# Token projection over pairs of rows with staggered softplus; patch filter with depthwise rows split between two engines

## The chip, the cores and the metric

The program runs on one core of one Trainium2 chip. The metric is device microseconds from start to end of one execution. The engines are TensorE (PE), VectorE (DVE), ScalarE (ACT), GpSimd (POOL) and SyncE (SP, which here issues nearly all DMAs). Each works through its own instructions in order; semaphores alone tie them together.

## The reference, cut to what matters

An image of 48 channels by 128x128 pixels goes through four layers, each `x = x + layer(group_norm(x))`: attention over all pixels, a patch filter, a selective scan and a box filter. The change touches the second layer and the first part of the third.

```python
# layer 1, patch filter: 48 -> 288 channels
y = einsum('oc,bchw->bohw', w_in, x)
f = rfft2(8x8 patches of y) * fft_mask;  y = irfft2(f)
y = depthwise 3x3 convolution of y (288 channels)
x1, x2 = split(y, 2)                      # 144 channels each
return einsum('oc,bchw->bohw', w_out, gelu(x1) * x2)
# layer 2, scan: a token is a 2x2 window, 192 numbers; 4096 tokens
Bm = tokens @ W_B.T + b_B;  Cm = tokens @ W_C.T + b_C
dt = softplus(tokens @ W_dt.T + b_dt);  delta = softplus(dt + b_dt)
# then the recurrence over tokens with delta, delta*u, Bm, Cm
```

## The kernel before, in words

**Group norm** (`group_norm`, used ahead of each layer): one `bn_stats` of VectorE per 512 pixels, two tiny matmuls, some tiny vector operations; it leaves scale and shift in `norm`. With `write_normalised` it also writes the normalised image to partitions 0 to 47 (`LO`) beside the original on 64 to 111 (`HI`). It is a block of its own: all engines meet at its start and at its end.

**Patch filter** (`patch_filter_layer`). After the norm, one block clears tiles on GpSimd and loads weights, a second prepares the mask and nine diagonal matrices (`diag`) on VectorE, and a third does the work. The image is worked off in 16 rows of patches (r), each in two halves (hf). For a half, `stage` (VectorE) writes normalised pixels to `staged_x`, TensorE transposes them (L739), VectorE copies them out (`x_t`, L920), TensorE applies the forward transform (L745, `ps_x`), ScalarE copies (`spec`, L810), TensorE mixes channels (L751, `ps_y`, four matmuls over two banks), VectorE multiplies by the mask (`ym`, L926), and TensorE transforms back (L758, `ps_i`) in three groups of channels: a and b of 128 and c of 48. ScalarE writes them to the slabs (`placed`, L824) with two rows of the slab above (`halos`, L831).
The depthwise convolution runs one row of patches later: group a (channels before the gelu) on TensorE, nine taps of 512 columns for each half (L770); groups b (128 channels, the gates) and c (the small third: 16 channels before the gelu and their 16 gates, on 48 partitions) on VectorE, each nine operations of 1024 elements (`taps`, L881, L883). `gates` multiplies gelu by gate, `output` multiplies by `w_out`, `add` adds to the image. VectorE's order is written out by hand: `iteration` gives away eight taps between a half's copy and its mask. A float32 matmul is two instructions in the profile.

**Token projection** (`project_tokens`). A block of norm with the normalised image written out; then a block in which GpSimd clears weight tiles, SP loads them and stores the image (`kept_image`), and then eight blocks of 512 tokens. A projection sums four matmuls, one for each place of the 2x2 window; eight projections a block (two halves of `dt`, two of `u`, four of `ps_b`). The softplus is |x|, exp(-|x|), ln(1+.), relu on ScalarE and an add on VectorE, done twice for each half, one after the other, through the same tiles. VectorE then splits delta and delta*u into three bfloat16 parts, and SP stores them (`parts`), from which the scan loads.

Of the kernel before, what the change touches and what calls it, by code (L numbers as in the profile page):

```python
# [19 lines left out]
BF16 = mybir.dt.bfloat16  # L20
# [70 lines left out]
def group_norm(nc, tag, image, gmean, norm, sems, write_normalised):  # L91


    with ExitStack() as ctx:
# [20 lines left out]
        def _(dve):  # L115
# [30 lines left out]
            if write_normalised:  # L146
                for px in quarters[:2]:
                    nc.vector.tensor_scalar(image[LO, px], image[HI, px], rstd, shift,
                                            ALU.mult, ALU.add).then_inc(normalised, 1)
                dve.wait_ge(normalised, written + 4)  # L150

# [480 lines left out]
PATCH = 8  # L632
HID = 3 * C
# [4 lines left out]
WP = W + 2  # L638


def patch_filter_layer(nc, image, gmean, norm, sems, ident, d):
# [5 lines left out]
    group_norm(nc, "gn1", image, gmean, norm, sems, False)  # L647
    with ExitStack() as ctx:
# [6 lines left out]
        dwa = n.sb("dwa", [P, 9])  # L655
        dwb = n.sb("dwb", [P, 9])
        dwc = n.sb("dwc", [SPAN, 9])
        diag = n.sb("diag", [P, 9, P])
        w_oa = n.sb("w_oa", [P, C])
        w_oc = n.sb("w_oc", [P, C])  # L660
# [6 lines left out]
        slab_c = n.sb("slab_c", [48, 2, SLAB, WP])  # L667
        gate_a = n.sb("gate_a", [P, 2, BLK])
        gate_c = n.sb("gate_c", [P, 2, BLK])
        acc_b = n.sb("acc_b", [P, PATCH, W])  # L670
        acc_c = n.sb("acc_c", [48, PATCH, W])
        ps_t = n.ps("ps_t", [P, 4, C])
# [4 lines left out]
        ps_o = n.ps("ps_o", [C, BLK])  # L677
        loaded, cleared, made = n.sem("loaded"), n.sem("cleared"), n.sem("made")
        staged, turned, turned_copied, spectrum, spectrum_copied, mixed, masked, inverted, placed, halo = (
            n.sem(s) for s in ("staged", "turned", "turned_copied", "spectrum", "spectrum_copied", "mixed", "masked",  # L680
                               "inverted", "placed", "halo"))
        conv_a, tap_b, tap_c, gelu_a, gelu_c, gated, product, added = (
            n.sem(s) for s in ("conv_a", "tap_b", "tap_c", "gelu_a", "gelu_c", "gated", "product", "added"))

        with nc.Block() as block:
            @block.sync
            def _(sp):
                pairs = ((fwd[:, :], d["fourier_fwd"]), (inv[:, :], d["fourier_inv"]),
                         (mask[0:64, :], d["mask"]), (mask[64:P, :], d["mask"]),
                         (mask2[0:64, :], d["mask_mirror"]), (mask2[64:P, :], d["mask_mirror"]),  # L690
                         (dwa[:, :], d["w_dw"][0:P, :]), (dwb[:, :], d["w_dw"][HID:HID + P, :]),
                         (w_oa[:, :], d["w_out"][0:P, :]))
                for dst, src in pairs:
                    sp.dma_start(dst, src).then_inc(loaded, 16)
                sp.wait_ge(cleared, 9)
                sp.dma_start(w_in[LO, :], d["w_in"]).then_inc(loaded, 16)
                sp.dma_start(dwc[0:REST, :], d["w_dw"][P:HID, :]).then_inc(loaded, 16)
                sp.dma_start(dwc[32:48, :], d["w_dw"][HID + P:2 * HID, :]).then_inc(loaded, 16)
                sp.dma_start(w_oc[32:48, :], d["w_out"][P:HID, :]).then_inc(loaded, 16)
                sp.wait_ge(loaded, 16 * 13)  # L700

            @block.gpsimd
            def _(pool):
                for t in (slab_a, slab_b, slab_c):
                    nc.gpsimd.memset(t[:, :, :, :], 0.0).then_inc(cleared, 1)
                nc.gpsimd.memset(gate_c[:, :, :], 0.0).then_inc(cleared, 1)
                nc.gpsimd.memset(w_oc[:, :], 0.0).then_inc(cleared, 1)
                nc.gpsimd.memset(acc_c[:, :, :], 0.0).then_inc(cleared, 1)
                nc.gpsimd.memset(dwc[:, :], 0.0).then_inc(cleared, 1)
                nc.gpsimd.memset(w_in[:, :], 0.0).then_inc(cleared, 1)  # L710
                nc.gpsimd.memset(spec[:, :, :], 0.0).then_inc(cleared, 1)

        with nc.Block() as block:
            @block.vector
            def _(dve):


                nc.vector.tensor_tensor(mask[:, :], mask[:, :], mask2[:, :], ALU.add).then_inc(made, 1)
                dve.wait_ge(made, 1)
                nc.vector.tensor_scalar(mask[:, :], mask[:, :], 0.5, None, ALU.mult).then_inc(made, 1)  # L720
                for t in range(9):
                    nc.vector.tensor_scalar(diag[:, t, :], ident[:, :], dwa[:, t:t + 1], None,
                                            ALU.mult).then_inc(made, 1)
                dve.wait_ge(made, 11)

        block = ctx.enter_context(nc.Block())
        rows_of = lambda slab, ph: slab[:, ph]
        final_rows = 1

        @block.tensor  # L730
        def _(pe):
            def transform(r, hf, first_work, second_work):

                q = r * 2 + hf
                pe.wait_ge(staged, q + 1)
# [1374 lines left out]
```

## Time and profile before

| | us |
|---|---|
| time, median of 3 runs | 8075.75 (8073.62 to 8077.5) |
| the profiled execution | 8077.16, its span 8075.4 |
| first and last mask of the patch filter | 3364.6 and 3890.3 |
| end of the second norm's statistics | 3976.6 |
| token projection's first matmul | 3994.6 |
| scan's first load issued | 4236.4 |

| stretch, us from the span's start | what it is |
|---|---|
| 0 to 3317 | attention |
| 3318 to 3342 | norm ahead of the patch filter |
| 3342 to 3948 | patch filter |
| 3948 to 3977 | norm ahead of the scan layer |
| 3977 to 4236 | token projection |
| 4236 to 7130 | scan |
| 7130 to 8075 | box filter |

Over the span PE is busy 80%, DVE 86%, ACT 65% and POOL 42%. These are averages over stages with different limits, so a stage must be read by itself; a PE that is busy is not a PE at its peak, since matmuls overlap.

### The profile page before, as it was taken

What the parts mean: (1) busy time and instruction counts of PE and PEld (TensorE: products, weight loads), DVE (VectorE), ACT (ScalarE), POOL (GpSimd) and SP (SyncE); (2) the same over time, 40 slices, a digit from 0 to 9 for tenths busy, and PEclk for the clock granted to TensorE, in tenths of its full rate; (3) what the DMA queues carried; (4) which work ended last, traced back from release to release, by engine and by line L of the source; (5) the groups of instructions that cost most, each with busy time, mean ns of one, the idle gap of its engine ahead of it and who ended that gap; (6) DMA issues with size and microseconds to landing.
All of it is one profiled execution on the core that took longest, in us unless ns stands there. A gap on an engine that the chain in (4) does not pass through costs nothing. (4 is left out here: it accounts for less than half of the span.)

```text
span 8075.4 us, 153634 instructions
## 1 busy us (share of the span) xinstructions
PE 6464.9 (80%) x60643; PEld 2907.0 (36%) x61152; DVE 6964.3 (86%) x6264; ACT 5223.3 (65%) x5277; POOL 3370.7 (42%) x1726
## 2 busy tenths in 40 slices
PE   4999999999999999799697777777777777733231
PEld 2534444444444444355233333333333333322110
DVE  7789999999999999788649999999999999954556
ACT  2178888888888888322278888888888888810000
POOL 1000000000000000000009999999999999825667
PEclk9999999999999999899899999999999999966665
DMA  1020000000000000000120000000000000022222
GB/s 27 26 41 6 5 5 5 7 5 5 5 7 5 5 5 5 3 0 0 27 57 6 6 6 7 6 6 6 7 6 6 6 6 6 5 73 65 66 67 76
DMA packets 116951, 138.49 MB, mean 17 GB/s; under 512 B 49885, under 2 KB 96061, under 8 KB 115149
## 3 DMA queue, kind: packets, MB, share of 16 engines
q1 hardware_dynamic: 91488, 76.06, 3.8%
q0 software_dynamic: 24576, 50.36, 2.4%
q8 instruction: 458, 7.50, 0.4%
q10 hardware_dynamic: 256, 3.15, 0.3%
q14 instruction: 173, 1.41, 0.1%
HBM read 93.83 MB, written 35.65 MB: 16 GB/s over the span
## 5 line engine op out<-in xcount | busy, mean ns | idle before, releaser
L1461 POOL TENSOR_TENSOR k_image<-k_image,s_b 128x1024 f32<-128x1024 f32 x1152 | 2700.8, 2355 | 356.0 <-ACT k_image L1379 321.5
L593 ACT ACTIVATE att_prob<-att_scores,a_bound,a_temp 128x1024 f32<-128x1024 f32 x2048 | 2320.5, 1201 | 558.2 <-PE att_scores L542 558.0
L604 DVE TENSOR_TENSOR att_prob_lo<-att_prob 128x1024 f16<-128x1024 f32 x2048 | 2434.8, 1237 | 252.4 <-ACT att_prob L593 235.1
L542 PE MATMUL att_scores<-att_queries,att_keys 64*128 64x512 f16 x12288 | 1447.3, 378 | 19.3 <-DMA att_keys<-qk_halves 19.3
L527 POOL TENSOR_TENSOR k_image<-k_image,att_rden 48x512 f32 x32 | 65.9, 2060 | 3162.2 <-DVE att_rden L616 3162.2
L1379 ACT COPY k_image<-h_du 128x1024 f32<-128x1024 f32 x1152 | 1167.0, 1013 | 322.7 <-PE h_du L1313 322.3
L1424 DVE TENSOR_TENSOR_SCAN h_state_odd<-h_keep,k_image 128x1024 f32<-128x1024 f32 x576 | 1319.8, 2325 | 0.2 <-ACT h_keep L1385 0.2
L1385 ACT ACTIVATE h_keep<-h_keep,h_decay 128x1024 f32<-128x1024 f32 x1152 | 1256.7, 1091 | 74.1 <-PE h_keep L1302 50.2
L1302 PE MATMUL h_keep<-h_rows,h_spread 128*128 128x512 bf16 x2303 | 698.6, 385 | 512.0 <-DVE h_state_odd L1424 263.3
L554 PE MATMUL att_sums<-att_prob,a_values 128*64 128x512 bf16 x8192 | 1056.5, 391 | 0.0
L542 PEld LDWEIGHTS att_scores<-att_queries,att_keys 64*128 64x128 f16 x12288 | 544.4, 94 | 878.3 <-issue 313.8
L1313 PE MATMUL h_du<-h_rows,h_spread 128*128 128x512 bf16 x1796 | 585.6, 385 | 105.0 <-issue 80.4
L1424 DVE TENSOR_TENSOR_SCAN k_image<-h_keep,h_state_odd,k_image 128x1024 f32<-128x1024 f32 x288 | 659.9, 2325 | 0.0
L1424 DVE TENSOR_TENSOR_SCAN k_image<-h_keep,k_image 128x1024 f32<-128x1024 f32 x288 | 642.6, 2265 | 8.2 <-POOL k_image L1461 7.3
L1647 POOL DMA_INDIRECT b_shared<-cells,b_index x512 | 506.7, 990 | 334.3 <-issue 147.6
L554 PEld LDWEIGHTS att_sums<-att_prob,a_values 128*64 128x64 f16 x8192 | 400.6, 108 | 602.0 <-issue 288.9
L561 PE MATMUL att_sums<-att_prob_lo,a_values 128*64 128x512 f16 x4096 | 554.1, 378 | 0.0
L1302 PEld LDWEIGHTS h_keep<-h_rows,h_spread 128*128 128x128 bf16 x2304 | 133.1, 97 | 1076.5 <-DVE h_state_odd L1424 489.3
L1697 PE MATMUL b_ps_t<-k_ident,b_mean 128*48 128x128 f32 x128 | 33.5, 417 | 581.9 <-DVE b_mean L1813 437.5
L1730 ACT ACTIVATE b_act<-b_ps_c,b_b,b_back 112x512 f32<-112x512 f32 x32 | 24.9, 777 | 643.1 <-remote 336.2
L1331 PE MATMUL h_y<-h_state_odd,s_c 128*32 128x192 f32 x4096 | 325.3, 337 | 1.5 <-DVE h_state_odd L1424 1.5
L1331 PE MATMUL h_y<-k_image,s_c 128*32 128x192 f32 x4096 | 324.0, 336 | 0.0
(275 smaller groups left out, 7236.6 us busy)
## 6 DMA issues: line engine op xcount, KB each, us to landing
y_rows<-h_y_sb SPq DMA_DIRECT2D x1024, 3.0 KB
att_queries<-qk_halves SPq DMA_DIRECT2D x256, 48.0 KB, 1.9
parts<-t_part SPq DMA_DIRECT2D x48, 192.0 KB, 2.5
h_rows<-parts SPq DMA_DIRECT2D x128, 72.0 KB
b_shared<-cells,b_index POOLq DMA_INDIRECT x512
att_keys<-qk_halves SPq DMA_DIRECT2D x64, 96.0 KB, 6.8
cells<-b_shared SPq DMA_DIRECT2D x4, 1536.0 KB, 5.1
qk_halves<-qkv_hi SPq DMA_DIRECT2D x32, 112.0 KB, 1.8
```

The costliest lines, as they stand in the source:

```text
L542: last = nc.tensor.matmul(scores[:, u % BATCH, r * BLK:(r + 1) * BLK], keys[part, j, g * KT:(g + 1) * KT], queries[part, slot, j, :], star ...
L554: nc.tensor.matmul(sums[part, slot, :], values[:, r * UNITS + g, part], prob_hi[:, u % RING, r * BLK:(r + 1) * BLK], start=g == 0 and r == ...
L561: last = nc.tensor.matmul(sums[r * CHUNK:(r + 1) * CHUNK, slot, :], values[:, r * UNITS + g, 0:CHUNK], prob_lo[:, u % RING, r * BLK:(r + 1 ...
L593: nc.scalar.activation(prob[:, u % RING, :], scores[:, u % BATCH, :], ACT.Exp, bias=bound[:, 0:1], scale=temp[:, 0:1]).then_inc(prob_ready, 1)
L604: nc.vector.tensor_tensor(prob_lo[:, u % RING, :], prob[:, u % RING, :], prob_hi[:, u % RING, :], ALU.subtract).then_inc(low_ready, 1)
L1302: last = nc.tensor.matmul(keep[:, k % 2, cols], spread[:, 0, slot, :], rows[:, c % 2, cols], start=True, stop=True)
L1313: last = nc.tensor.matmul(du[:, cols], spread[:, 1, slot, :], rows[:, c % 2, cols], start=True, stop=True)
L1331: last = nc.tensor.matmul(out, b_c[stat][:, c * CH + t0:c * CH + t0 + TB], h[:, s0:s0 + d1 - d0, t0:t0 + TB], start=stat == 2, stop=stat == 4)
L1379: nc.scalar.copy(du_sb[k % 3], du[:, :]).then_inc(du_copied, 1)
L1385: nc.scalar.activation(keep[:, k % 2, :], keep[:, k % 2, :], ACT.Exp, scale=decay[:, ds(g * SLOTS + k // STEPS * SLOTS + k % SLOTS, 1)]).t ...
L1424: nc.vector.tensor_tensor_scan(out=state[c % 2][:, slot, :], data0=keep[:, k % 2, :], data1=drive[k % 3], initial=initial, op0=ALU.mult, o ...
L1461: nc.gpsimd.tensor_tensor(drive[k % 3], du_sb[k % 3], b[:, c * CH:(c + 1) * CH], ALU.mult).then_inc(drive_ready, 1)
```

## The change

It has four parts. (1) In the patch filter, loads, clears and the preparation of mask and `diag` move into the norm's block, on SP and GpSimd (`beside_sync`, `beside_pool`). The attention layer is wrapped in a clean-up that frees its semaphores. (2) In the loop, TensorE convolves six of the eight rows of group a (`ps_d` four rows, `ps_m` two) and VectorE the other two (`acc_a`). Group c is laid out as two halves of four rows, on partitions 0 to 47 and 64 to 111, so its VectorE operations have 512 elements and not 1024; a further copy (`join`) gives the lower half its upper neighbours. Staging and the copy `x_t` go from VectorE to ScalarE. The nine taps of TensorE are shared out as 2, 2, 0 and 5 over the four places beside the transforms of a row. The output of a row is made in one go, three matmuls of 512 columns instead of four. (3) The normalised image is no longer written out by the norm; VectorE and ScalarE write it so that rows of even and odd y lie on `LO` and `HI`, and a projection sums two matmuls instead of four. Loads, clears and the store of the image move into the norm's block. (4) The two softplus are staggered: a step does the second one of block i-1 together with the first one of block i, over tiles of both halves. The third bfloat16 part is made by GpSimd.

```diff
+        def prepare(pool):
+            ... memsets of w_oc, dwc, w_in, slabs, gate_c, spec
+            pool.wait_ge(loaded, 16 * 16)
+            nc.gpsimd.tensor_tensor(mask[:, :], mask[:, :], mask2[:, :], ALU.add).then_inc(made, 1)
...
+        group_norm(nc, "gn1", image, gmean, norm, sems, False, beside_sync=load_weights, beside_pool=prepare)
...
+TAPS_BESIDE = ((range(0, 2), range(2, 4)), (range(0), range(4, TAPS)))
+                    for out, row0, nrow in ((ps_d, 0, HALF), (ps_m, HALF, PE_ROWS - HALF)):
...
-                pe.wait_ge(masked, q * 4 + 4)
+                        if b == 0:
+                            pe.wait_ge(masked, q * 4 + t + 1)
...
+                for part, y0 in ((upper, 0), (lower, HALF)):
+                    for t in range(4):
+                        last = nc.tensor.matmul(out_rows, ym[:, t, 2 * P:MIX], rows_of[:, :, y0:y0 + HALF, :],
+                                                start=True, stop=True)
...
+            def iteration(r, ph, out=True):
+                k, kph = r - 1, 1 - ph
+                for t in range(2):
+                    taps(k, kph, t)
+                if out:
+                    gates(r - 2, ph)
+                tap_c_rows(k, kph, 2)
+                tap_a_rows(k, kph, 2)
+                mix(r, 0)
+                tap_b_rows(k, kph, 2)
+                for t in range(3, 5): ...
+                ... add(r - 2), taps 5 and 6
+                mix(r, 1)
+                for t in range(7, TAPS): ...
...
-                    for place in range(4):
+                for b in range(WIN):
...
+            def step(i):
+                second_absolute(i - 1)
+                first_absolute(i)
+                exponentials(i, levels)
+                copy_stats(i, (0, 1))
+                logarithms(i, levels)
+                copy_stats(i, (2, 3))
...
+            with pe.Fori(1, nblk - 1) as i:
+                stats(i)
+                deltas(i + 1)
+                inputs(i)
...
+            with dve.Fori(2, nblk) as i:
+                soften(i)
+                finish(i - 1)
+                rectify(i)
...
+                    pool.wait_ge(split, i * 6 + half * 3 + 3)
+                    nc.gpsimd.tensor_tensor(rest[:, half, :, :], rest[:, half, :, :], part[:, half, 1, :, :],
+                                            ALU.subtract).then_inc(low_split, 1)
+                    nc.gpsimd.tensor_copy(part[:, half, 2, :, :], rest[:, half, :, :]).then_inc(low_split, 1)
```

The first place is TensorE in the patch filter's loop, half 1 of a row of patches: `ps_y` is the mix, `ps_i` the transform back, `ps_d` and `ps_m` the depthwise taps, `ps_o` the output. Before:

```order
L739 MATMUL p_ps_t<-k_ident,p_staged_x 128x48 x4
...
L777 MATMUL p_ps_o<-p_gate_a,p_w_oa 48x512
L778 MATMUL p_ps_o<-p_gate_c,p_w_oc 48x512
L745 MATMUL p_ps_x<-p_fwd,p_x_t 48x128 x4
...
L770 MATMUL p_ps_d<-p_slab_a,p_diag 128x512 x9
...
L751 MATMUL p_ps_y<-p_w_in,p_spec 128x304 x2
...
L758 MATMUL p_ps_i<-p_inv,p_ym 128x128 x8
...
L758 MATMUL p_ps_i<-p_inv,p_ym 48x128 x4
```

Now, the same half of a row:

```order
L772 MATMUL p_ps_y<-k_ident,p_staged_x 128x48 x4
...
L759 MATMUL p_ps_o<-p_gate_c,p_w_oc 112x512
L761 MATMUL p_ps_o<-p_gate_a,p_w_oa 48x512 x2
L781 MATMUL p_ps_x<-p_fwd,p_x_t 48x128 x4
L750 MATMUL p_ps_d<-p_slab_a,p_diag 128x512
L750 MATMUL p_ps_m<-p_slab_a,p_diag 128x256
...
L788 MATMUL p_ps_y<-p_w_in,p_spec 128x304 x2
...
L796 MATMUL p_ps_i<-p_inv,p_ym 128x128 x2
...
L796 MATMUL p_ps_i<-p_inv,p_ym 128x128 x5
...
L806 MATMUL p_ps_i<-p_inv,p_ym 48x64 x8
...
L772 MATMUL p_ps_y<-k_ident,p_staged_x 128x48 x4
```

The output of two halves stands in one place now, the taps of 512 columns have taps of 256 beside them, and the transform back of group c is eight matmuls of 64 columns.

The second place is ScalarE in the loop over blocks of tokens. Before, the first softplus of a half and the second behind it (`t_sp_ln` feeds `t_both` on VectorE, which this engine waits for in between):

```order
L1123 ACTIVATE t_sp_abs<-t_ps_dt,t_bias_dt 96x512
...
L1126 ACT_TABLE_LOAD
L1126 ACTIVATE t_sp_exp<-t_sp_abs 96x512
L1129 ACT_TABLE_LOAD
L1129 ACTIVATE t_sp_ln<-t_sp_exp 96x512
L1130 ACTIVATE t_sp_pos<-t_ps_dt,t_bias_dt 96x512
L1123 ACTIVATE t_sp_abs<-t_both,t_bias_dt 96x512
...
L1126 ACT_TABLE_LOAD
L1126 ACTIVATE t_sp_exp<-t_sp_abs 96x512
L1129 ACT_TABLE_LOAD
L1129 ACTIVATE t_sp_ln<-t_sp_exp 96x512
L1130 ACTIVATE t_sp_pos<-t_both,t_bias_dt 96x512
```

Now one step of the loop, as far as its second table load:

```order
L1260 ACTIVATE t_second<-t_once,t_bias_two 96x512 x2
...
L1253 ACTIVATE t_first<-t_ps_dt,t_bias_dt 96x512 x2
...
L1266 ACT_TABLE_LOAD
L1266 ACTIVATE t_second<-t_second 96x1024
...
L1266 ACTIVATE t_first<-t_first 96x1024
...
L1278 ACTIVATE s_b<-t_ps_b,t_bias_bc 128x512
...
L1278 ACTIVATE s_b<-t_ps_b,t_bias_bc 128x512
...
L1271 ACT_TABLE_LOAD
L1271 ACTIVATE t_second<-t_second 96x1024
L1271 ACTIVATE t_first<-t_first 96x1024
```

Both halves and both softplus share one load of the exponential's table and one of the logarithm's, and two of the copies out of `ps_b` stand between them.

## Rows read from the trace of the kernel before

**Rows 1.** Busy us and count of each engine, granted clock (of 1), by stretch.

```profile
3342.00:3380.00 38.00, 17.05 (x88) 12.05 (x88) 8.70 (x24) 4.11 (x7) 9.33 (x9) 0.66 0.06 15
3414.00:3620.00 206.00, 196.39 (x793) 108.52 (x791) 178.55 (x205) 47.61 (x85) 0.00 (x0) 1.00 0.00 0
3995.00:4230.00 235.00, 232.12 (x512) 89.63 (x510) 112.61 (x141) 186.80 (x232) 0.00 (x0) 0.99 0.23 61
4230.00:7130.00 2900.00, 2237.25 (x30821) 997.12 (x31331) 2835.14 (x1728) 2416.86 (x2562) 2700.78 (x1152) 0.98 0.04 9
```

**Rows 2.** Timeline (start, us, engine, line): DVE, masks ending rows 0 and 15.

```profile
3375.99 0.99 DVE L926 TENSOR_TENSOR p_ym<-p_ps_y,p_mask 128x304 f32<-128x304 f32 x2 [0.36 <-PE p_ps_y L751]
...
3889.76 0.99 DVE L926 TENSOR_TENSOR p_ym<-p_ps_y,p_mask 128x304 f32<-128x304 f32 x2 [0.46 <-PE p_ps_y L751]
```

**Rows 3.** Timeline of PE, half 1 of a row of patches.

```profile
3612.58 2.63 PE L751 MATMUL p_ps_y<-p_w_in,p_spec 112*128 112x304 f32 x8
3615.86 3.05 PE L758 MATMUL p_ps_i<-p_inv,p_ym 128*128 128x128 f32 x24 [0.64 <-DVE p_ym L926]
...
3620.96 1.04 PE L745 MATMUL p_ps_x<-p_fwd,p_x_t 128*48 128x128 f32 x8
3621.93 8.00 PE L770 MATMUL p_ps_d<-p_slab_a,p_diag 128*128 128x512 f32 x18
3629.76 1.19 PE L751 MATMUL p_ps_y<-p_w_in,p_spec 112*128 112x304 f32 x4
```

**Rows 4.** Timeline: PE, `ps_b` of one block; SP, the scan's first load.

```profile
4011.21 14.54 PE L1094 MATMUL t_ps_b<-k_image,t_w_bc 112*128 112x512 f32 x32
...
4236.41 0.38 SPq L1229 DMA_DIRECT2D h_decay<-in_a_log  x1
```

**Rows 5.** Groups of ACT, tokens: operation | busy, mean ns | idle before.

```profile
L1126 ACT ACT_TABLE_LOAD x32 | 41.1, 1283 | 0.6
...
L1126 ACT ACTIVATE t_sp_exp<-t_sp_abs 96x512 f32<-96x512 f32 x32 | 20.2, 630 | 0.4
```

**Rows 6.** Timeline, end of each norm and the first work behind it.

```profile
3341.78 0.16 DVE L143 SCALAR_TENSOR_TENSOR k_norm<-gn_work,k_norm 48x1 f32<-48x1 f32 x1
...
3358.83 0.55 DVE L912 TENSOR_SCALAR p_staged_x<-k_image,k_norm 48x512 f32<-48x512 f32 x1 [0.88 <-PEq L713]
...
3976.47 0.16 DVE L143 SCALAR_TENSOR_TENSOR k_norm<-gn_work,k_norm 48x1 f32<-48x1 f32 x1
...
3994.62 1.99 PE L1094 MATMUL t_ps_dt<-k_image,t_w_dt 112*96 112x512 f32 x2 [19.57 <-DMA t_skip_w<-in_skip]
```

**Rows 7.** Timeline, the end of the patch filter.

```profile
3929.34 1.94 PE L777 MATMUL p_ps_o<-p_gate_a,p_w_oa 128*48 128x512 f32 x2 [16.00 <-DVE p_gate_c L897]
...
3938.78 2.28 PE L799 MATMUL p_ps_d<-p_slab_a,p_diag 128*128 128x128 f32 x18 [1.31 <-DVE p_slab_a L961]
...
3947.20 0.28 DVE L904 TENSOR_TENSOR k_image<-p_ps_o,k_image 48x128 f32<-48x128 f32 x1 [1.18 <-PE p_ps_o L778]
```

**Rows 8.** Timeline of DVE, patch filter: a first tap, two neighbouring taps.

```profile
3620.77 0.73 DVE L881 TENSOR_SCALAR p_acc_b<-p_slab_b,p_dwb 128x1024 f32<-128x1024 f32 x1
...
3625.84 1.27 DVE L883 SCALAR_TENSOR_TENSOR p_acc_b<-p_slab_b,p_dwb,p_acc_b 128x1024 f32<-128x1024 f32 x1
3627.03 1.27 DVE L883 SCALAR_TENSOR_TENSOR p_acc_c<-p_slab_c,p_dwc,p_acc_c 48x1024 f32<-48x1024 f32 x1
```

**Rows 9.** Timeline of DVE, tokens: last sum of a softplus to last subtraction.

```profile
4011.83 0.69 DVE L1167 TENSOR_TENSOR t_both<-t_sp_pos,t_sp_ln 96x512 f32<-96x512 f32 x1 [5.28 <-ACT t_sp_pos L1130]
...
4016.63 1.22 DVE L1184 TENSOR_TENSOR t_rest<-t_rest,t_part 96x1024 f32<-96x1024 f32 x1
```

**Rows 10.** Store of the image, from issue to landing.

```profile
DMA to landing us min/median/max: 6.9/15.2/24.9
```

**Rows 11.** Attention: duration ns min/median/max, first and last start, forms.

```profile
L527 POOL TENSOR_TENSOR k_image<-k_image,att_rden x32: 1259/2082/2101, 585.2 to 3316.2; 48x512 f32 x32
...
L604 DVE TENSOR_TENSOR att_prob_lo<-att_prob x2048: 1207/1220/2315, 426.3 to 3305.7; 128x1024 f16<-128x1024 f32 x187
```

## What the change will do: the prediction

> **What bounds the kernel now.** I read the busy times by stretch first, then the timeline of TensorE in one half of a row of patches, then VectorE's, and last the joints between stages.
>
> In the patch filter's loop TensorE is busy 196.4 of 206 us at clock 1.00, VectorE 178.6, ScalarE 47.6 [rows 1]. TensorE is the bound, with VectorE close behind. From the mask that ends row 0 (3376.98) to the one that ends row 15 (3890.75) are 15 rows, 34.25 us each [rows 2]. One half takes 17.18 [rows 3]: 3.28 from the first mix to the transform back, 5.10 for transform back (3.05), transposes and output, 0.97 forward, 7.83 taps.
>
> In the token projection TensorE is busy 232 of 235 us [rows 1]; 32 instructions take 14.54, 0.449 each [rows 4], so the 64 of a block take 28.8. The table loads, 41.1 us for one function of two [rows 5], lie beside that. ScalarE is the next limit, with 187 us.
>
> At the joints nearly everything stands still: 16.9 us from the end of the first norm (3341.94) to the first staging, 18.0 from the second's (3976.63) to the first matmul [rows 6]. From there to the scan's first load, 4236.41 [rows 4], the layer takes 259.8 from its norm.
>
> **Joint 1.** GpSimd's clears and SP's loads go under the norm's 24 us. GpSimd had 9.3 us of clears in this stretch [rows 1]; the clears are somewhat smaller now, and with mask and `diag` I estimate 12, so about 8 us of cover are left. If the cover were gone, the block would end that much later. What is late next is the entry of the loop's block, 0.9 us by the idle time in front of the first staging [rows 6]. 16.9 becomes 0.9, a gain of 16.0; group c's longer transform (below), twice, takes 0.8 back: 15.2. The clean-up behind attention is a GpSimd instruction and a meeting of all engines, which no row shows; between 0.9 (one block entry) and 3 I take 1.5, added.
>
> **The loop.** A tap on TensorE was two instructions of 0.435 (7.83 / 18). Now it is two of 0.435 and two of 256 columns, for which I take half, 0.22 (18 of 128 columns take 2.28, 0.127 each [rows 7], so short ones do get cheaper); at worst they cost 0.435. Nine taps: 11.8 instead of 15.7. Output: 6 instructions, 2.6, instead of 8, 3.5. Transform back: a and b as before, 16 x 0.127 = 2.0; group c is now 16 instructions of 64 columns instead of 8 of 128. By columns they cost 1.0 in all, by the 0.13 of an instruction with 48 weight columns (8 in 1.04 [rows 3]) 2.1; I take 1.95, near that row. The transform back no longer waits for all four masks: only its last matmul waits, so it ends 0.13 + 0.26 + 1.02 + 1.95 = 3.4 behind the last mask.
>
> VectorE: operations of 1024 follow each other at 1.19 [rows 8]. 0.96 elements a ns make 1.067 of this, so 0.128 is fixed: 512 elements cost 0.66, 256 cost 0.395. A tap over c, a and b costs 2.25, against 2.39. First taps are about twice as fast (0.73 long), 1.33 for three. Gates 2.0 (was 2.5), adds 1.4, masks 4.3 to 4.6; staging and `x_t` (1.8) leave for ScalarE, which has room for them. In all about 27 instead of 30.
>
> Now the two halves of a row, from last mask to last mask. Half 1: TensorE transforms back 3.4, transposes 0.4, output 2.6, forward 1.0, five taps 6.5, mix until its last mask 3.15 (3.28 less 0.13): 17.0. VectorE has 11.7 of taps and adds here, and waits. Half 0: TensorE 3.4 + 0.4 + 2.6 (taps 0 and 1) + 1.0 + 2.6 (taps 2 and 3) + 3.15 = 13.1; VectorE two taps 4.5, first taps 1.3, a tap 2.25, gates 2.0, c and a of tap 2 1.05, four masks 2.3 (0.99 the pair [rows 2], and 0.3 of waits) = 13.4, so VectorE sets it, by a little. A row: 30.45 instead of 34.25, times 15: **57.0 gained**. Bounds of the row: 29.6 with group c cheap, 32.4 to 33 with dear short taps. TensorE's handovers are covered: `x_t` lies under taps or output of 2.6, the copy `spec` under 2.6 or 6.5.
>
> **The loop's end.** From 3890.75 to 3947.48 [rows 2, 7] are 56.7. Now: taps 7 and 8 (4.5), the last row's taps (19.3), gates 2.0, output at the low clock 5.3 (1.94 for two instructions [rows 7], 0.87 apart), adds 1.4, gates 2.0, output 5.3, adds 1.4, clears 0.6, the last pixel row with b and c interleaved 4.7, then gate, output and add 2.3: 48.8. Gained 7.9.
>
> **Token projection.** TensorE now has 32 instructions a block, 14.4 us. ScalarE has nine short operations of 0.65 to 0.7, four passes of 1024 at 1.07 and two loads of 1.28: 13. But the staggering closes a chain. `inputs(i)` of half 1 waits until VectorE has read the one before it (`skipped`), and `stats(i+1)` is queued behind it on TensorE. The loop: inputs 1.8, two of the `ps_b` 3.6, copy 0.8, table load 1.28 [rows 5], two logarithms of 1024 2.1 (twice the 0.63 of an exponential of 512 [rows 5], less one fixed part, some 0.2), `soften` 1.55, `finish` of half 0 4.8 (4011.83 to 4016.63 are its operations as they were [rows 9]), half 1 as far as skip 2.2, a handover 0.1: **18.3 us a block**. Nothing else is near it: VectorE's own work is 12.
>
> The layer from the norm: entry and pairing of rows 2.9; first `dt` 5.8, at the low clock first; step 0 until its logarithm 6.7; step 1 15.9, whose `inputs` waits for nobody; six steps 109.5; `soften`, `finish(6)`, `rectify`, `finish(7)` 21.7, the two `finish` 9.7 each; 2.4 in which GpSimd stands in VectorE's way (next paragraph); GpSimd's last part 3.9; store and the scan's start 3.2. Sum 172, against 259.8: **87.8 gained**. It holds 15 of joint 2. The store of the image landed 6.9 to 24.9 us behind its issues [rows 10]; under a norm of 29 us it is covered by about 7.
>
> GpSimd beside VectorE: a tensor_tensor of 512 elements took 1.26 on GpSimd with VectorE still, 2.08 in the median beside it; VectorE's own of 1024, 1.22 in the median, rose to 2.32 [rows 11]. So the two shut each other out. In a step GpSimd starts half 0's third part when VectorE is already in half 1's first sum, and while it holds (2.4), VectorE's next two operations read PSUM and one tile. [...]
>
> The Trainium skill, ScalarE: Activation LUTs, What ACT_TABLE_LOAD costs, gives 2.66 us for a switch, a drain of 1.38 being added to the load. Here the load takes 1.283, and the exponential behind it sat idle 0.4 us in 32 times [rows 5]: no drain is seen. With the page's price the one load in the chain would cost 1.4 more a block, 8 in six steps.
>
> **Sum.** 15.2 - 1.5 + 57.0 + 7.9 + 87.8 = 166.4 from the profiled 8077.2: 7910.8. The median of the runs is 1.4 lower than the profiled execution; I say 7910. The scan and the box filter are the same code.
>
> **Rivals.**
> *A, short matmuls are cheap.* Group c's transform costs 1.0 by its columns. Half 1 then is 16.1, half 0 stays with VectorE at 13.4: 29.5 a row, 14 more: 7896. For it: 0.127 at 128 columns. Against: 0.13 with 48 weight columns looks like a floor. 20%.
> *B, the short ones are dear and handovers uncovered.* 256 columns at up to 0.435, or VectorE and TensorE, now both over 27 of 30 us, stall each other: 32.9 a row, 37 less: 7947. For it: the row has no slack on either. 14%.
> *C, GpSimd in the chain.* If its operation begins before VectorE's first sum of half 1, or blocks PSUM readers also, each step is 2.4 longer, and perhaps twice: six or seven steps, 15 to 33 less, 7925 to 7943. For it: [rows 11]. 15%.
> *D, the preparations don't fit.* The norm's blocks end late, up to what they save, 30: 7940. The covers are 8 and 7 us. 3%.
> *E, the other side.* TensorE's clock. It held 1.00, 2.4 GHz, through the loop [rows 1]; where it had waited 16 us, two instructions were 1.94 long, about twice the usual: 1.2 GHz [rows 7]. Should the new waits in the loop let it fall, about 24 us of a row's 28 of work become 48: plus 24 for each row at the low clock, so from 7 such rows the change loses; with all 15, 8270. Against it: the scan keeps 0.98 with TensorE busy 77% [rows 1]. 1%.
> Forecast: 47%.
>
> **The numbers.** This kernel's measurement tells 0.2% (16 us) from no change. All but E are 130 us or more faster. Faster 0.98, same 0.01, slower 0.01. The range takes in A (with room for a row of 28.8 to 7880) and most of B and C: 7880 to 7955.
>
> **What would show it.** Right: a row of patches of about 30.5 between masks; half 1 about 17 and half 0 13.4; tap instructions of 256 columns 0.22 apart; a block of tokens 18.3 with TensorE waiting for `skipped`; 18 table loads in the projection; 1 us between norm and first staging; scan's first load 172 behind the norm. Wrong: a row above 32 or below 29.5, VectorE's sums of 0.7 stretched beyond 2 in each step, a granted clock under 0.95 in the loop, or a changed scan.

## The result, and the profile after

The changed kernel takes 7865.5 us in the median of 4 runs (7860.6 to 7867.0), the kernel before 8074.7: a ratio of 0.974, 95% interval [0.972, 0.976]. Two later batches gave 0.9737 [0.972, 0.975] and 0.9740 [0.973, 0.975]. The forecast was 7910, from 7880 to 7955: the direction was right, but the gain is 209 us where 166 were forecast, and the time lies 14 us below the range. By the two profiled executions (spans 8075.4 and 7862.6):

| piece, us | before | after | gained | forecast |
|---|---|---|---|---|
| as far as the end of norm 1 | 3341.9 | 3342.4 | -0.5 | -1.5 |
| to the mask that ends row 0 | 35.0 | 18.8 | 16.3 | 15.2 |
| 15 rows of patches | 513.8 | 421.9 | 91.9 | 57.0 |
| to the patch filter's last add | 56.7 | 45.8 | 10.9 | 7.9 |
| norm 2 | 29.2 | 24.5 | 4.7 | 0 |
| to the scan's first load | 259.8 | 176.1 | 83.7 | 87.8 |
| scan and box layer | 3839.0 | 3833.1 | 5.9 | 0 |

The loop's stretch now, as [rows 1] showed it (us, busy us and count of PE, PEld, DVE, ACT, POOL, granted clock):

```profile
3414.00:3611.00 197.00, 188.67 (x1021) 124.00 (x1020) 182.00 (x272) 73.43 (x147) 0.00 (x0) 1.00 0.00 0
3858.00:4024.00 166.00, 125.24 (x256) 45.12 (x254) 117.27 (x131) 104.09 (x124) 56.81 (x31) 0.91 0.24 72
```

VectorE has moved up to 182 of 197 us, TensorE is at 189, and the clock stays at 1.00, as in [rows 1]. In the projection TensorE is down to 125 of 166, no longer what bounds it; its clock is 0.91 in the mean there. The masks that end rows 0 and 15, as in [rows 2], lie 421.9 us apart, 28.13 a row:

```profile
3360.20 0.99 DVE L1010 TENSOR_TENSOR p_ym<-p_ps_y,p_mask 128x304 f32<-128x304 f32 x2 [0.36 <-PE p_ps_y L788]
...
3782.11 0.99 DVE L1010 TENSOR_TENSOR p_ym<-p_ps_y,p_mask 128x304 f32<-128x304 f32 x2 [0.46 <-PE p_ps_y L788]
```

Beside [rows 3], TensorE's timeline around one last mask of half 0 (its end is 3569.75) and up to the next:

```profile
3567.94 1.29 PE L788 MATMUL p_ps_y<-p_w_in,p_spec 112*128 112x304 f32 x4 [1.08 <-DVE p_ym L1010]
3569.07 2.11 PE L796 MATMUL p_ps_i<-p_inv,p_ym 128*128 128x128 f32 x16
3571.11 0.91 PE L806 MATMUL p_ps_i<-p_inv,p_ym 128*48 128x64 f32 x16
3571.95 0.45 PE L772 MATMUL p_ps_y<-k_ident,p_staged_x 48*128 48x48 f32 x4
3572.33 1.11 PE L759 MATMUL p_ps_o<-p_gate_c,p_w_oc 128*112 128x512 f32 x2
3573.37 1.06 PE L761 MATMUL p_ps_o<-p_gate_a,p_w_oa 128*48 128x512 f32 x4
3574.27 1.04 PE L781 MATMUL p_ps_x<-p_fwd,p_x_t 128*48 128x128 f32 x8
...
3581.80 2.63 PE L788 MATMUL p_ps_y<-p_w_in,p_spec 112*128 112x304 f32 x8
```

Half 1 goes from 3569.75 to 3584.94, 15.19 us, and TensorE has no gap in it. Group c's way back (L806) is 16 instructions in 0.84 us (to the start of the next), the output 2 in 1.04 and 4 in 0.90. The single starts in the trace say more: within each of group c's two parts the instructions follow each other at 0.056 us, and the second part begins 0.27 us behind the first, beside it; the four of L761 start in two pairs, 0.01 us apart in a pair and 0.47 from pair to pair. Half 0 is 13.12, and there TensorE waits 1.08 for a mask. VectorE in that place, with the prices that [rows 8] led to:

```profile
3564.62 1.22 DVE L988 TENSOR_TENSOR p_gate_a<-p_gate_a,p_acc_b 128x1024 f32<-128x1024 f32 x1
...
3566.36 0.75 DVE L960 SCALAR_TENSOR_TENSOR p_acc_c<-p_slab_c,p_dwc,p_acc_c 112x512 f32<-112x512 f32 x1
3567.02 0.48 DVE L960 SCALAR_TENSOR_TENSOR p_acc_a<-p_slab_a,p_dwa,p_acc_a 128x256 f32<-128x256 f32 x1
...
3568.76 0.99 DVE L1010 TENSOR_TENSOR p_ym<-p_ps_y,p_mask 128x304 f32<-128x304 f32 x2 [0.49 <-PE p_ps_y L788]
...
3582.60 0.89 DVE L1010 TENSOR_TENSOR p_ym<-p_ps_y,p_mask 128x304 f32<-128x304 f32 x2 [1.09 <-PE p_ps_y L788]
```

512 elements cost 0.66 (3566.36 to 3567.02), both gates 1.74. VectorE goes without a pause into the masks of half 0, and stands 1.09 us ahead of those of half 1.

The joint of norm 1 [rows 6] and the second norm's loop now, and behind them that loop in the kernel before:

```profile
3342.26 0.15 DVE L143 SCALAR_TENSOR_TENSOR k_norm<-gn_work,k_norm 48x1 f32<-48x1 f32 x1
3342.99 0.81 ACT L840 ACTIVATE p_staged_x<-k_image,k_norm 48x512 f32<-48x512 f32 x1 [1.71 <-PEq L94]
...
3829.80 19.17 DVE L117 BATCH_NORM_STATS2 gn_stats<-k_image  x32 [0.85 <-PEq L661]
```

```profile
3949.39 22.79 DVE L117 BATCH_NORM_STATS2 gn_stats<-k_image  x31 [0.38 <-issue]
```

A step of the projection on VectorE, from one `soften` (L1318) to the next (3922.96):

```profile
3904.84 1.40 DVE L1318 SCALAR_TENSOR_TENSOR t_once<-t_ps_dt,t_bias_neg,t_first 96x512 f32<-96x512 f32 x2 [3.43 <-ACT t_first L1271]
...
3912.93 1.24 DVE L1346 CAST t_part<-t_both 96x1024 bf16<-96x1024 f32 x1
3914.20 1.94 DVE L1349 TENSOR_TENSOR t_rest<-t_both,t_part 96x1024 f32<-96x1024 f32 x1
...
3916.78 2.75 DVE L1326 TENSOR_SCALAR t_pos<-t_once,t_bias_two 96x512 f32<-96x512 f32 x2
3922.96 1.41 DVE L1318 SCALAR_TENSOR_TENSOR t_once<-t_ps_dt,t_bias_neg,t_first 96x512 f32<-96x512 f32 x2 [3.43 <-ACT t_first L1271]
```

TensorE in the same step, and the group of the projection's exponentials' table loads (operation | busy, mean ns | idle before):

```profile
3905.87 3.83 PE L1206 MATMUL t_ps_dt<-k_image,t_w_dt 112*96 x8 [1.63 <-DVE t_once L1318]
...
3913.15 2.01 PE L1206 MATMUL t_ps_u<-k_image,t_w_u 112*96 x4 [1.66 <-DVE t_skip L1342]
```

```profile
L1266 ACT ACT_TABLE_LOAD x9 | 11.5, 1283 | 0.2
```

The steps are 18.1 us but for one of 19.7 (110.2 for six, from 3886.83 to 3997.03, 18.4 in the mean); TensorE waits 1.66 for `skipped`, in the place that the prediction named. In the step of 19.7 its granted clock is 0.50, 1.2 GHz, for 3.4 us right behind that wait (us, busy us of PE, PEld, DVE, ACT, POOL, clock):

```profile
3951.03:3954.44 3.41, 3.41 (x5) 1.33 (x4) 3.38 (x4) 2.85 (x3) 1.52 (x2) 0.50 0.39 123
```

The changed kernel's repeats (`after_again`, `after_b`) have none and two such steps, each with such a stretch, so its projection takes 173.8 to 177.6 us from run to run. GpSimd's third part does hold VectorE up, but behind the second skip: a cast takes 1.24 us where it takes 0.68 alone, a subtraction 1.94 for 1.22, and the second of the two operations of `rectify` (L1326) 2.35 for 0.48. The product and the skip before them, which read PSUM (L1339, L1342), stay at 0.69 and 0.74 beside it.

### The profile page after: what moved, and what is told of

It is laid out like the page before. It is cut to its first block and busy times, and to the rows that moved or that the text cites. A ratio compares the mean times of both kernels' runs of the same rounds, so it can differ in the third digit from the quotient of the medians.

```text
span 7862.6 us, 153992 instructions
## 1 busy us (share of the span) xinstructions
PE 6351.9 (81%) x61120; PEld 2861.0 (36%) x61120; DVE 6898.8 (88%) x6320; ACT 5176.6 (66%) x5280; POOL 3423.9 (44%) x1770
## 5 line engine op out<-in xcount | busy, mean ns | idle before, releaser
L1492 PE MATMUL h_du<-h_rows,h_spread 128*128 128x512 bf16 x2304 | 700.3, 386 | 36.1 <-DMA h_rows<-parts 33.6
```

Of the source, the lines that this page charges most:

```text
L1492: last = nc.tensor.matmul(du[:, cols], spread[:, 1, slot, :], rows[:, c % 2, cols], start=True, stop=True)
```

## The experiments

Each kernel is the changed one with one edit unless said otherwise. "Changed" is its time in the same batch. The batch of the first four runs was 1.5% faster than all others, before included (7950 us), with the difference in the box layer (from the end of norm 3, 785 to 792 us against 895 to 913), for which nothing here gives a cause; there "changed" is 0.9739 of it, 7743, and what the two traces show of an edit is the surer number. The batch of `mask_all`, `third_on_dve` and `best` had no changed kernel in it either.

**One part alone.** `patch_only` has the projection of before, `tokens_only` the patch filter of before.

> The patch filter of the changed kernel with the projection, and the second norm, of the kernel before. Theory (the parts add up): the two traces give the patch filter 118.6 us of the 212.8 us between them (first norm -0.5, joint 16.3, rows 91.9, loop's end 10.9), so 8074.7 - 118.6 = 7956 us; the 4.7 us of the second norm and the 5.9 us behind the first load of the scan go with one part or the other: the second norm's statistics take 0.60 us each if they follow the patch filter's code, 0.735 us if they follow the norm's own form. Rival (the parts lean on each other, as by what state they leave): the time is more than 8 us away from 7956.

> The projection of the changed kernel, with its second norm, behind the patch filter of the kernel before. Theory (the parts add up): 83.7 us between the end of the second norm and the first load of the scan, so 8074.7 - 83.7 = 7991 us; with both of the unexplained pieces (4.7 and 5.9 us) 7980 us. Rival: the steps of the projection are not 18.4 us a block here, because something of the patch filter was needed for them.

Measured 7841.4 (108.7 gained) and 7865.7 (84.4), 193.1 together, where both parts give 207. `tokens_only` is as expected; `patch_only` gains 9.9 less than its 118.6, past the 8 us that its rival named. The pieces agree with the table to 3 us (rows 421.9 in the one, projection 173.8 in the other). Most of what the sum lacks is behind them: in `patch_only` the third norm's loop took 24.19 us, 5 too many, and its box layer 6.7 more than in `tokens_only`. So no sign is seen that the parts lean on each other. And norm 2's gain goes with the patch filter's code, though nothing in the norm reads it:

```profile
7018.62 24.19 DVE L117 BATCH_NORM_STATS2 gn_stats<-k_image  x32 [1.22 <-PEq L1545]
```

```profile
3950.49 23.57 DVE L117 BATCH_NORM_STATS2 gn_stats<-k_image  x32 [1.22 <-PEq L662]
```

**The loop of statistics.** The kernel before, with eight small memsets ahead of that loop in norm 2:
```diff
+            for column in range(8 if tag == "gn2" else 0):
+                nc.vector.memset(pad[HI, column:column + 1], 0.0)
             with dve.Fori(0, nst) as i:
...
```


> The kernel before with eight one-column memsets (0.06 us each) ahead of the loop of statistics in the second norm alone. Theory P1 (where the loop lies in VectorE's program sets its pace: 32 steps took 23.5 us there and 19.17 us in every other norm of the kernel before): the loop may fall to 19.17 us with nothing else changed. Rival P2 (the state that the patch filter leaves, or the image's data, sets it): 23.5 us again, as in both kernels with the patch filter of before.

```profile
3948.63 19.17 DVE L120 BATCH_NORM_STATS2 gn_stats<-k_image  x32 [0.25 <-issue]
```

19.17 us: P2 falls, since patch filter and image are those of the kernel before. What had changed are the eight memsets and the tile that they write to. (The whole, one run of 8071.7 beside 8059 to 8078, can't show 4 us.) So norm 2's 4.7 us are a by-product of the code around the loop, and `patch_only` met the same in norm 3. P1, the loop's place in VectorE's program, fits all of this. It is not shown by itself: the memsets also take some time ahead of the loop, and their tile is one more in SBUF.

**The output's halves.** Weights of group a padded with zeros to 112 columns:
```diff
-    last = nc.tensor.matmul(ps_o[64 * hh:64 * hh + C, 0:ncol], w_oa[:, :], ...
+    last = nc.tensor.matmul(ps_o[0:m, 0:ncol], w_oa[:, hh, 0:m], ...
```


> The changed kernel with the output's two matmuls of group a over all 112 output columns each (zeros in the columns of the other half), so that they can't run side by side. Theory M1 (the output was cheap because its two halves lie on different output columns of TensorE and ran together: 4 instructions in 0.90 us): they take 1.8 us again, the part of the row that TensorE sets grows from 15.2 to about 16.1 us, 13 us over 15 rows and about 2 us at the loop's end: 7880 us. Rival M2 (they were cheap for another reason, such as short weights): no change, 7865 us, and four instructions again in 0.9 us.

```profile
3578.86 1.11 PE L762 MATMUL p_ps_o<-p_gate_c,p_w_oc 128*112 128x512 f32 x2
3579.81 1.88 PE L764 MATMUL p_ps_o<-p_gate_a,p_w_oa 128*112 128x512 f32 x4
3581.62 1.07 PE L785 MATMUL p_ps_x<-p_fwd,p_x_t 128*48 128x128 f32 x8
```

7755.2, some 12 more: M1. The four instructions take 1.81 instead of 0.90, the rows are 12.0 us longer (433.9) and the loop's end 2.4. The edit widens the weights too, but narrow weights alone don't make the output cheap (M2): in the kernel before, two instructions with 48 columns of weights took 0.90 by themselves.

```profile
3619.21 1.06 PE L777 MATMUL p_ps_o<-p_gate_a,p_w_oa 128*48 128x512 f32 x2
3620.11 1.02 PE L778 MATMUL p_ps_o<-p_gate_c,p_w_oc 128*48 128x512 f32 x2
```

On output columns of their own two matmuls ran at the same time.

**Group c's data columns.**
```diff
-    last = nc.tensor.matmul(out_rows, ym[:, t, 2 * P:MIX], rows_of[:, :, y0:y0 + HALF, :], ...
+    last = nc.tensor.matmul(ps_i[part, use % 2, t * P:(t + 1) * P], ym[:, t, 2 * P:MIX], inverse[:, :], ...
```


> The changed kernel with 128 columns instead of 64 in each of the 8 matmuls that bring group c back from frequencies, in both parts (a second inverse with its rows of pixels turned, whose other half nobody reads): same instructions, double columns. Theory C1 (a float32 matmul with 48 columns of weights costs by its own columns, 0.053 us an instruction at 64): 0.107 to 0.127 us an instruction, so 0.87 to 1.2 us more per half row; the half that TensorE sets pays it (15.2 to 16.1 to 16.4 us), the other one has 1.08 us of waiting to hide it: 13 to 20 us, 7878 to 7885 us. Rival C2 (a price by the instruction, as the forecast took it with 0.12 us each): no change, 7865 us.

```profile
3562.31 0.75 PE L808 MATMUL p_ps_i<-p_inv,p_ym 128*48 128x128 f32 x5
...
3562.90 0.27 PE L808 MATMUL p_ps_i<-p_inv,p_ym 128*48 128x128 f32 x1
3562.94 0.27 PE L808 MATMUL p_ps_i<-p_inv_low,p_ym 128*48 128x128 f32 x1
...
3563.80 0.45 PE L777 MATMUL p_ps_y<-k_ident,p_staged_x 48*128 48x48 f32 x4
```

7755.2, some 12 more; the rows are 10.3 us longer (432.2), 0.64 each but for the first. C2 falls. C1 holds in its price, 0.109 us from start to start within a part where it was 0.056, but the 16 take 1.49 us, 0.65 more a half, less than C1 asked. The rows show why: where the second part (`inv_low`, output columns 64 to 111) follows the first, matmuls of the two start 0.04 apart, side by side, and these are about half of each part.

**Both.**

> The changed kernel with both edits at once: group a's output over 112 output columns, and 128 columns in group c's way back. Theory (the two prices that the forecast had too high are all of the miss in the half that TensorE sets): one edit took that half from 15.2 us by 0.9 us, the other by 0.65 us; together 16.75 us, near the 17.0 of the forecast, and 25 us more than the changed kernel (ratio to before 0.977). Rival (the two are hidden by one and the same wait, or the half turns to another bound): clearly less than the sum, 12 to 15 us.

7888.2 against 7861.7, 26.5 more; rows 444.2 instead of 421.9, and half 1 is 16.69 us. The prices add up: this is a kernel with what the forecast thought it would pay, and it lies 22 us from the forecast's 7910.

**Group c's weights.** Part one gets 112 columns of weights, 64 of them zeros:
```diff
-    for part, y0 in ((upper, 0), (lower, HALF)):
+    for part, width, y0 in ((slice(0, SPAN), SPAN, 0), (lower, C, HALF)):
-        last = nc.tensor.matmul(out_rows, ym[:, t, 2 * P:MIX], ...
+        last = nc.tensor.matmul(out_rows, ym[:, t, 2 * P:2 * P + width], ...
```


> The changed kernel with 112 instead of 48 columns of weights (64 of them zeros) in the first part of group c's way back; the second part, which then writes its own output columns over the zeros, stays at 48. The data columns stay 64 in both. Theory F1 (the forecast's price by the instruction holds where weights are wide, since they must be loaded for each matmul; narrow weights took it away): the 8 instructions of the first part take 0.10 to 0.12 us each, those of the second 0.053 us: 0.4 to 0.5 us more in each half, 6 to 8 us in all (ratio 0.9745). Theory F2 (64 data columns cost 0.053 us whatever the weights): no change.

```profile
3562.64 1.53 PE L807 MATMUL p_ps_i<-p_inv,p_ym 128*112 128x64 f32 x16
3564.10 0.45 PE L773 MATMUL p_ps_y<-k_ident,p_staged_x 48*128 48x48 f32 x4
```

7871.1 against 7863.1, 8.0 more: F1. The 16 take 1.46 us instead of 0.84, and the single starts show what this is made of. The eight with wide weights follow each other at 0.098 (3562.64 to 3563.33), the narrow eight behind them at 0.056 as before. That is 0.3 us; the rest is that the first part now covers the second one's output columns, so that the second no longer runs beside it but starts 0.19 behind its last. So there is a floor, near 0.10, and it belongs to wide weights; the narrow ones pay by their data. With 128 data columns it doesn't show: 0.112 with 128 columns of weights (L796), 0.109 with 48 (L781). Width is not all of it: the transposes (L772), with weights of 128 columns over only 48 partitions, start 0.06 apart; no run looks into that.

**One wait for all masks.**
```diff
-    if b == 0:
-        pe.wait_ge(masked, q * 4 + t + 1)
+    if b == 0 and t == 0:
+        pe.wait_ge(masked, q * 4 + 4)
```


> The changed kernel with one wait for all four masks ahead of the first group's matmuls back, as in the kernel before, instead of a wait for each. Theory W1 (in the half that TensorE sets, its matmuls back start 0.7 us ahead of the end of the last mask, and that is time of the row): that half goes from 15.2 to 15.9 us, the other one hides it in its 1.08 us of waiting: 10 to 11 us slower than the changed kernel (ratio to before 0.975). Rival W2 (the start is early, but the next wait of the half takes it back): no change.

```profile
3566.32 2.05 PE L796 MATMUL p_ps_i<-p_inv,p_ym 128*128 128x128 f32 x16 [0.57 <-DVE p_ym L1010]
```

7876.1, ratio 0.976 against 0.974; rows 432.8, 10.9 longer, and half 1 is 15.86: W1.

**VectorE's third tap behind the masks.**
```diff
-                tap_c_rows(k, kph, 2)
-                tap_a_rows(k, kph, 2)
                 mix(r, 0)
-                tap_b_rows(k, kph, 2)
+                taps(k, kph, 2)
```


> The changed kernel with VectorE's third tap of groups c and a (0.67 and 0.38 us in a row of taps) put behind the first half's masks instead of ahead of them. Theory S1 (the first half is set by VectorE, on which TensorE waits 1.08 us, while VectorE stands idle 1.1 us ahead of the second half's masks): the first half gets 1.05 us shorter, the second stays with TensorE: 1.0 us a row, 15 us in all, and VectorE then nowhere idle over 0.5 us. Rival S2 (what counts is VectorE's whole row, since the gates and the adds hand over late): no change or a gain under 4 us.

7849.9 against 7861.7, 11.8 less, the rows 12.9 less (409.0): S1. Half 0 is 12.19 now, half 1 still 15.19, and TensorE has no wait left in either; the 1.05 us that VectorE gave up were cut at 0.93 by TensorE's own work. TensorE's timeline in half 0, all four mixes in one row now, and the way back; the 1.08 us of idle time between the mixes are gone:

```profile
3560.47 2.63 PE L788 MATMUL p_ps_y<-p_w_in,p_spec 112*128 112x304 f32 x8
3562.94 2.11 PE L796 MATMUL p_ps_i<-p_inv,p_ym 128*128 128x128 f32 x16
```

**The third part of the split on VectorE.**
```diff
+    nc.vector.tensor_tensor(rest[:, half, :, :], rest[:, half, :, :], part[:, half, 1, :, :],
+                            ALU.subtract).then_inc(low_split, 1)
...
+    nc.vector.tensor_copy(part[:, half, 2, :, :], rest[:, half, :, :]).then_inc(low_split, 1)
```

> The changed kernel with the third part of the split on VectorE again, as before, and GpSimd without work in the projection. Theory G1 (GpSimd's part is off the chain): VectorE gets 3.8 us of work more a block and is shut out 2.7 us less, so its load goes from 14.7 to 15.8 us, under the step of 18.1 us: the step stays, and the whole is within 3 us of the changed kernel. Rival G2 (the exclusion costs the chain, the forecast's rival C): 5 us or more gained. Rival G3 (VectorE's load is what the step follows): 1 us a block, 7 us or more lost.

7888.3, ratio 0.978; the traced execution, the fastest of the four (7874.0 to 7893.2), has a projection of 198.0, 22 more. The loss has G3's sign, but none of the three mechanisms: the steps are 21.5 and 22.8 us in turn, while VectorE idles 6.2 and 7.5 of them. Half 0's third part (1.22 and 0.69) is now queued ahead of half 1's sum and skip, on which ScalarE's second absolute value and TensorE's inputs wait:

```profile
3914.19 1.22 DVE L1339 TENSOR_TENSOR t_rest<-t_rest,t_part 96x1024 f32<-96x1024 f32 x1
...
3916.06 0.68 DVE L1322 TENSOR_TENSOR t_both<-t_pos,t_second 96x512 f32<-96x512 f32 x1
...
3917.38 0.74 DVE L1328 TENSOR_SCALAR t_skip<-t_ps_u,t_skip_w 96x512 f32<-96x512 f32 x1
...
3929.68 1.41 DVE L1304 SCALAR_TENSOR_TENSOR t_once<-t_ps_dt,t_bias_neg,t_first 96x512 f32<-96x512 f32 x2 [6.21 <-ACT t_first L1257]
```

TensorE's wait for the skip grows from 1.66 to 3.41 us, and behind it the granted clock is 0.50 in every step, for 3.4 and 6.8 us in turn, where the three traces of the changed kernel have one, none and three such stretches in six steps. Half 1's inputs take 3.28 and 3.70 us for 2.01 (TensorE's timeline in one step, then the clock in two):

```profile
3918.26 3.28 PE L1192 MATMUL t_ps_u<-k_image,t_w_u 112*96 x4 [3.41 <-DVE t_skip L1328]
```

```profile
3918.73:3922.14 3.41, 3.41 (x5) 1.22 (x4) 3.29 (x4) 3.38 (x5) 0.00 (x0) 0.50 0.39 115
3939.21:3946.04 6.83, 6.29 (x8) 2.51 (x9) 5.60 (x8) 4.99 (x6) 0.00 (x0) 0.50 0.43 126
```

The six steps are 24.4 us longer than six of 18.1. The longer wait is 10.5 of it, 1.75 a step; the other 14 are put down to the low clock as what is left, an estimate.

**Sums, products and skips first.**
```diff
+    for half in range(2):
+        nc.vector.tensor_tensor(both[:, half, 0, :], pos[:, half, :], second[:, half, :], ...
+    for half in range(2):
+        nc.vector.tensor_tensor(both[:, half, 1, :], ps_u[:, half, :], both[:, half, 0, :], ...
+        nc.vector.tensor_scalar(skip[:, half, :], ps_u[:, half, :], ...
     for half in range(2):
...
```


> The changed kernel with the finishing of a block of tokens in another order on VectorE: sums, products and skips of both halves first, then the splits of both (the tiles for it are doubled). Theory T1 (the step of 18.1 us is the chain logs, soften, finish as far as the second half's skip, inputs, statistics, copy, table, logs; TensorE waits 1.66 us in it for that skip): the wait goes and the step is 16.5 us, 10 to 12 us in all. Rival T2 (VectorE's load with GpSimd's third part beside it, 14.7 us and longer where the two exclude each other, or ScalarE's 13.9 us, sets the step): under 4 us gained, since the exclusion grows.

7853.3 against 7861.7, 8.4 less; projection 165.1 against 173.8. T1: a step is 16.25 us, and TensorE's inputs (the last row) run through. The six steps give 11.1 us, of which the entry and the end take 2.4 back. TensorE waits once in a step now, 1.64 us for `soften`, and not twice, and the six steps hold no stretch at the low clock in any of the three traces with this order (`early`, `best`, `best_b`).

```profile
3904.49 1.41 DVE L1318 SCALAR_TENSOR_TENSOR t_once<-t_ps_dt,t_bias_neg,t_first 96x512 f32<-96x512 f32 x2 [0.77 <-ACT t_first L1271]
...
3912.93 3.04 DVE L1351 TENSOR_TENSOR t_rest<-t_both,t_part 96x1024 f32<-96x1024 f32 x1
...
3920.74 1.41 DVE L1318 SCALAR_TENSOR_TENSOR t_once<-t_ps_dt,t_bias_neg,t_first 96x512 f32<-96x512 f32 x2 [0.67 <-ACT t_first L1271]
```

```profile
3909.19 3.76 PE L1206 MATMUL t_ps_u<-k_image,t_w_u 112*96 x8
```

The exclusion of the two engines did grow (3.04 us for the subtraction of half 1), still in VectorE's slack, of which 0.7 us are left.

**Both reorderings.**

> The changed kernel with both reorderings: VectorE's third tap behind the first half's masks, and the early sums, products and skips in the projection. Theory (they lie in different stages and add): 11.7 and 8.4 us, 20 us under the changed kernel, ratio to before 0.971. Rival: one of the two gains was noise of the runs, under 14 us.

> The changed kernel with both reorderings again. Theory (the gains add): 20 us under the changed kernel on the same chip. Rival (one is noise): under 14 us.

7842.2, ratio 0.972 [0.970, 0.973], and in the batch with the changed kernel beside it 7835.0 against 7863.1: 28 less, ratio 0.971 [0.969, 0.972]. By the traces 25.7: rows 409.0 and projection 164.9 instead of 421.9 and 177.6. That is more than the sum because this repeat of the changed kernel had two steps at the low clock; against `after_again`, which had none, the pieces give 21.8. It beats both kernels. The changed kernel's own repeats were `after_again` (7861.7) and `after_b` (7863.1).

## Why the prediction failed, and what in it was right

The direction held, and in the main the mechanisms; the size did not, and the time fell outside the range. **The loop** is the step that failed: 57.0 forecast, 91.9 measured. The two terms of TensorE's half of a row, group c's transform at 1.95 us and the output at 2.6, were taken too dear; they measured 0.84 and 1.94. Piece by piece:
- *Transform back, "group c ... I take 1.95, near that row"*: 0.84, 1.1 us a row. The row taken ([rows 3], 8 instructions in 1.04) was one of 128 data columns, where the price by columns and the supposed floor lie together; it could not show a floor for 64. `c_weights` shows one of 0.098 with 112 columns of weights and none with 48. This is rival A with its mechanism, and A's 1.0 for it was near; the last 0.2 are the two parts running side by side, which A had not.
- *Output, "6 instructions, 2.6"*: 1.94, 0.7 us a row. That two halves on different output columns run together stood in no term and no rival (`out_wide`).
- *Half 1, 17.0, set by TensorE*: 15.19. With these two corrections the forecast's own sum is 17.0 - 1.1 - 0.7 = 15.2; the taps of 256 columns (0.43 for two), the forward transform and the mix came as taken.
- *Half 0, 13.4, set by VectorE*: 13.12, and VectorE did set it; the gates take 1.74 instead of 2.0.
- *"A row: 30.45 instead of 34.25, times 15"*: 14 rows are 28.2 to 28.3, the first of them 25.8. No row two back exists for it, so it has no gates and no output.

A row of 28.3 lies under the 29.5 that the prediction gave as a sign of being wrong, and under rival A's as well.

Both could have been suspected beforehand. The Trainium skill, TensorE: Matmul & The Clock Gate, LDWEIGHTS (loading the stationary operand), puts the time of a weight load at its columns divided by 1.2 in ns: as an estimate 40 ns for 48 columns, under the 56 that the data take here, and 93 for 112. By that rule group c would cost by its data, as rival A had it. The trace agrees, with 98 ns from start to start for the wide ones. The same page of the Trainium skill, Part 3: Packing small matmuls — row/col tiling, lets matmuls run at the same time where their outputs start at different partitions, 2.4 times as fast for three of 32 columns. Here it was twice as fast for two of 48.

**Joint 1**, 15.2: right, 16.3; the preparations fit under the norm, and rival D fell. **The clean-up** cost 0.5, not 1.5. **The loop's end**, 7.9: 10.9. Of the 3.0 more, some 2.7 are the two outputs at the low clock, forecast at 5.3 each: six instructions took 3.9, since the four of L761 took 1.95, as two did before [rows 7]:

```profile
3808.75 2.05 PE L759 MATMUL p_ps_o<-p_gate_c,p_w_oc 128*112 128x512 f32 x2 [11.55 <-DVE p_gate_c L993]
3810.72 1.95 PE L761 MATMUL p_ps_o<-p_gate_a,p_w_oa 128*48 128x512 f32 x4
```

**The token projection**, 87.8: right in size (83.7) and mechanism. The chain of 18.3 is 18.1 in the trace, and `early` cut it at the named link. The 4 us too much are the entry (17.3 to the first `soften` instead of 15.4), the end (1.4) and the one step at the low clock. The 18 table loads take 1.283 each, with 0.2 us of idle time in all ahead of each nine and 0.1 behind them: no drain. **Rival C** fell in the changed kernel: the two engines shut each other out, but off the chain, and VectorE's two readers of PSUM were not held; what lies on the chain is VectorE's order. Of the operations with a single tile of SBUF as input, a cast and `rectify` were held as well, the latter to 2.35 in each step. **Rival B** and **E** fell: 28.3 us a row, and in the loop the clock stays at 1.00. But E looked at the loop alone. In the projection the clock did fall behind TensorE's waits, for which no term and no rival stood: once in the six steps here, in each step of `third_on_dve`.

**Norm 2**, nothing forecast, 4.7: a by-product of the code around it (`norm_shift`). **Scan and box layer**, 5.9: not shown to be an effect. From the scan's first load to the end of norm 3 all kernels but `patch_only` took 2923.9 to 2927.8, and the two profiled executions agree to 0.2; the box layer of unchanged code took 895 to 913 from one execution to the next.

So of the 46 us missed, 35 are in the rows, 4.7 in norm 2, 3 the loop's end, 5.9 scatter, 2 joint and clean-up, with 4 the other way in the projection. Of the rows' 35 the two prices are 27, half 0 is 4 and the short first row 2.5; the rest is rounding. Why code around it changes that one loop was not tried.

## What to carry to other kernels

A price for a small matmul must come from a row with the same width of weights and of data, and from the starts of its instructions, not from the length of the group, in which edges and neighbours are mixed: narrow weights took away a floor that wide ones show, and matmuls on separate output columns overlapped. When two engines alternate in setting a loop's halves, look for work of one that can cross the boundary: moving two taps was worth 12 us with nothing removed. In a staggered chain, what counts is the position of the instruction that others wait for, not an engine's load: 3.8 us of work a block on an engine with 3.4 idle cost 22 us, of which the longer wait itself is 10. And a wait of TensorE can cost more than itself: with waits of 1.63 and 1.66 us in a step the clock fell none to three times in six steps, with 1.63 and 3.41 in each step, with a single one of 1.64 never.

## What was not expected of the hardware

- Float32 matmul instructions with 48 columns of weights and 64 of data followed each other at 0.056 us, with 112 and 64 at 0.098.
- Two 512-column matmuls (four instructions) on output columns 0 to 47 and 64 to 111 took 0.90 us together, at the low clock 1.95; when both covered 0 to 111, 1.81.
- TensorE's granted clock was 0.50 for 3.4 to 6.8 us behind each wait of 3.41 us in `third_on_dve`, and behind some of those of 1.66 us in the changed kernel.
- A loop of 32 statistics on VectorE took 19.17 or 23.6 to 24.2 us, by the code around it.
- One subtraction of VectorE (1.22 us alone) took 3.04 beside GpSimd's in `early`, and an operation with one input in SBUF 2.35 for 0.48.
